# A transformer layer on one core: a fourth PSUM bank for the first group's experts, first loads on two queues, three items moved to the drain, and a new order of all items

## The reference

```python
x = x + attn(cond_moe(x))          # sparse experts, then banded linear attention, layer norm
x = x + ffn(cond2(x))              # 16-head attention with position bias and null key, then FFN

# cond_moe: 8 experts of 64 plus 2 shared, top 2 by routing
logits = (x @ wt.T + repeat(cond @ wg.T)) / 2 ; scores = softmax(logits)
y = sum_top2(w_e * ((leaky(x @ gate_e) * (x @ up_e)) @ down_e)) + shared(x)
# attn: qkv = y @ W + b ; out = (q k^T / scale * band) v ; layer norm
# cond2: xn = ln(x) * g ; q, k l2-normed ; softmax(8 q k^T + bias, causal, mask) v ; ln(out @ Wout)
# ffn: h = silu(z w1) * (z w2) ; h = gelu(h h1) ; h = gelu(h h2) ; h @ w3
```

## Time and profile before

| | |
|---|---|
| median of 3 runs | 853.04 us (852.45 to 853.72) |
| the profiled execution | 853.67 us, its span 851.9 us |
| PE busy | 800.9 us (94%), 5368 matmuls |
| PEld busy | 599.7 us (70%) |
| ACT busy | 603.0 us (71%) |
| DVE busy | 589.0 us (69%) |
| POOL busy | 447.4 us (53%) |
| DMA | 16.98 MB, mean 20 GB/s |
| mean granted clock | 0.992 |

### The profile page before, as it was taken

One profiled execution on the slowest core, in us unless ns is written; L12 is line 12 of the kernel. 1 busy time (PEld: TensorE's weight loads), 2 busy tenths in 40 slices (PEclk: granted clock), 3 DMA queues, 4 the chain that ended last, 5 costly groups with the idle time before them and its releaser, 6 DMA issues. The chain is left out here.

```text
span 851.9 us, 16700 instructions
## 1 busy us (share of the span) xinstructions
PE 800.9 (94%) x5368; PEld 599.7 (70%) x5368; DVE 589.0 (69%) x1581; ACT 603.0 (71%) x1649; POOL 447.4 (53%) x388
## 2 busy tenths in 40 slices
PE   5978879999999999999999999999999989999987
PEld 4756556678676777678676777778776766777777
DVE  5578878776767686776767586776767786664522
ACT  2314768588857888588866878588866978779944
POOL 3027874754558365754558364654558455944200
PEclk9989999999999999999999999999999999999999
DMA  7041100000010000100010000100010000000000
GB/s 245 1 156 35 63 14 4 2 2 2 1 41 2 1 2 2 42 1 2 2 42 1 2 1 2 41 1 1 1 42 1 2 1 2 13 2 1 13 7 7
DMA packets 15588, 16.98 MB, mean 20 GB/s; under 512 B 1408, under 2 KB 13072, under 8 KB 15120
## 3 DMA queue, kind: packets, MB, share of 16 engines
q1 hardware_dynamic: 15216, 15.27, 5.7%
q10 hardware_dynamic: 288, 0.66, 0.2%
HBM read 13.81 MB, written 2.11 MB: 19 GB/s over the span
## 5 line engine op out<-in xcount | busy, mean ns | idle before, releaser
L632 POOL TENSOR_TENSOR sb_sm<-sb_sm,sb_rden 128x512 f32<-128x512 f32 x128 | 135.9, 1068 | 209.0 <-DVE sb_rden L1097 209.0
L728 ACT ACTIVATE sb_sm<-sb_sm,sb_nmx 128x129 f32<-128x129 f32 x512 | 199.2, 393 | 26.7 <-DVE sb_nmx L1092 26.4
L1084 DVE SCALAR_TENSOR_TENSOR sb_sm<-ps_S,sb_rq,sb_biasm 128x129 f32<-128x129 f32 x512 | 140.9, 343 | 60.2 <-PE ps_S L1316 21.2
L625 POOL TENSOR_TENSOR sb_biasm<-sb_bias,sb_maskn 128x512 f32<-128x512 f32 x128 | 165.8, 1310 | 21.5 <-DVE sb_sm L1084 12.8
L615 POOL TENSOR_TENSOR sb_rq<-sb_qss,sb_mhalf 128x16 f32<-128x16 f32 x32 | 92.5, 2916 | 41.5 <-DVE sb_qss L1069 41.5
L728 ACT ACTIVATION_READ_ACCUMULATOR sb_sm<-sb_sm,sb_nmx 128x1 f32 x512 | 97.1, 190 | 0.0
L1316 PEld LDWEIGHTS ps_S<-sb_k,sb_qs 64*128 64x128 f32 x1024 | 64.8, 187 | 34.7 <-issue 32.9
L1316 PE MATMUL ps_S<-sb_k,sb_qs 64*128 64x129 f32 x1024 | 83.1, 291 | 6.5 <-DVE sb_sm L1084 6.5
L1092 DVE TENSOR_REDUCE sb_nmx<-sb_sm 128x4 f32<-128x516 f32 x128 | 85.8, 675 | 0.6
L735 ACT ACTIVATE sb_pT<-ps_T 128x512 f32<-128x512 f32 x128 | 75.0, 591 | 14.3 <-PE ps_T L1324 14.3
L1324 PE MATMUL ps_T<-sb_ident,sb_sm 128*128 128x128 f32 x512 | 76.8, 276 | 3.4 <-ACT sb_pT L735 2.4
(11 more groups left out here) (226 smaller groups left out, 1800.7 us busy)
## 6 DMA issues: line engine op xcount, KB each, us to landing
sb_xg<-in_xT SPq DMA_DIRECT2D x8, 256.0 KB, 4.2
sb_xs<-in_x SPq DMA_DIRECT2D x8, 256.0 KB, 3.8
sb_qs<-in_xT SPq DMA_DIRECT2D x1, 2048.0 KB, 10.8
sb_hA<-in_h SPq DMA_DIRECT2D x2, 1024.0 KB, 4.8
out_y<-sb_res SPq DMA_DIRECT2D x7, 256.0 KB, 2.6
sb_sm<-toeplitz SPq DMA_DIRECT2D x1, 1024.0 KB, 5.8
sb_rows<-in_rows SPq DMA_DIRECT2D x1, 648.0 KB, 6.8
sb_oT<-in_wq SPq DMA_DIRECT2D x1, 512.0 KB, 10.4
```

Source lines behind the costliest of these rows:

```text
L625: pool.tensor_tensor(biasm[:, heads, 1:NK], bias0[:, heads], maskn[:, j // 4].unsqueeze(1).broadcast_to([128, 4, S]), ALU.add)\
L632: pool.tensor_tensor(sm[:, heads, 1:NK], sm[:, heads, 1:NK], rden[:, heads].unsqueeze(2).broadcast_to([128, 4, S]), ALU.mult)\
L728: ins = act.activation(sm[:, h], sm[:, h], ACT.Exp, bias=nmx[:, h:h + 1], accum_out=den[:, h:h + 1])
L1084: ins = dve.scalar_tensor_tensor(sm[:, h], bank(g, "sim", n, odd)[:, m * NK:(m + 1) * NK], rq[:, k * HEADS + h:k * HEADS + h + 1], biasm[: ...
```

## The change

- PSUM: stage A of group 0 (it runs in the fill) takes its banks from a ring F, which is the ring M and the bank T1. `warm` uses T0.
- DMA: SP issues x's first group, then wg and wu, then cols and rows; condT, wgT and wt go to ScalarE's queue, where wg and wu were.
- GpSimd sets `eps` first and counts a semaphore of its own; ScalarE runs one copy of 128 x 1 on it, ahead of its wait for `cols`.
- `l3d.2`, `l3d.3` and `l4d.0` leave the last phase; `l3p.2`, `l3p.3` and `l4p.0` join the drain, on every engine that has a part in them.
- Every engine's list is in a new order in every phase. No other item is added or removed.

The diff, cut: of the 30 lists the ones below; the hunks behind them are whole.

```diff
@@ ORDER @@
     "pe fill": """
-        lg.0 warm.0-2 pb.0-1 warm.3-7 lg.1-2 rw.0 exp.0 lg.3-4 exp.1 lg.5 exp.2 lg.6-7 pb.2 warm.8 exp.3-4
-        warm.9 down.0 pb.3 warm.10-12 qkv.0 scores.0 warm.13 mix.0 warm.14 fl.0 warm.15 fl.1-2 warm.16 xnT.0
-        fl.3 q.0-2 warm.17 kv.0 q.3 qs.0-1 q.4-5 qs.2-3 q.6 qs.4 q.7 qs.5-7 warm.18 qst.0 warm.19-21 kT.0
+        lg.0 warm.0 pb.0 warm.1-5 pb.1 warm.6 lg.1-2 warm.7 rw.0 exp.0 lg.3-4 exp.1 lg.5 exp.2 lg.6 pb.2 lg.7
+        exp.3 warm.8 exp.4 down.0 warm.9 pb.3 warm.10 qkv.0 scores.0 mix.0 warm.11-13 fl.0-2 warm.14 fl.3 xnT.0
+        warm.15-16 q.0-2 kv.0 q.3 qs.0-2 q.4-7 qs.3-7 warm.17 qst.0 kT.0 warm.18-21
     """,
...
     "pe start": """
-        rw.0 sim.0 exp.0 sim.1 exp.1 sim.2 exp.2-3 PT.0 sim.3 PT.1 exp.4 PV.0 sim.4 PT.2 down.0 sim.5 PT.3 qkv.0
-        scores.0 PV.1 mix.0 PT.4 sim.6 PT.5-6 sim.7 PV.2 z.0-1 PT.7 sim.8 z.2 sim.9 PT.8-9 xnT.0 PV.3 PT.10
-        sim.10 q.0-1 sim.11 kv.0 q.2 PT.11 q.3 PT.12 PV.4 qs.0-2 q.4-5 z.3 q.6 qs.3 PT.13 z.4 qs.4-5 PV.5-6 q.7
-        PT.14 kT.0 PT.15 qs.6 z.5 qs.7 PV.7 qst.0 z.6-7
+        sim.0 rw.0 sim.1 exp.0-1 sim.2 exp.2 sim.3 exp.3 PT.0-1 exp.4 PV.0 sim.4 PT.2 down.0 PT.3 sim.5 PT.4
+        qkv.0 scores.0 PT.5 sim.6 PT.6 mix.0 PV.1 sim.7 z.0-1 PT.7 PV.2 sim.8 PV.3 z.2 PT.8 z.3 sim.9 PT.9 xnT.0
+        PV.4 PT.10 sim.10 q.0 kv.0 sim.11 PT.11 q.1-2 PT.12 q.3 PV.5 qs.0-2 z.4 q.4-5 PT.13 z.5 q.6-7 PT.14
+        qs.3-5 kT.0 PT.15 qs.6-7 PV.6-7 qst.0 z.6-7
     """,
...
     "pe steady": """
-        sim.0 rw.0 exp.0-1 sim.1 exp.2-3 sim.2 exp.4 down.0 PT.0 sim.3 zT.0 PT.1 qkv.0 l1.0 sim.4 l1.1 PT.2 l1.2
-        PT.3 PV.0-1 l1.3 sim.5 scores.0 z.0 l2.0-1 PT.4 sim.6 l2.2 PT.5-6 l2.3 mix.0 sim.7 l3.0-1 PT.7 l3.2
-        sim.8 PV.2-3 sim.9 z.1 PT.8 xnT.0 l3.3 PT.9 kv.0 q.0 PT.10 sim.10 q.1 z.2-3 q.2 PT.11 sim.11 PV.4-5
-        qs.0-1 q.3 PT.12 q.4 z.4 q.5 PT.13 l4.0 q.6 PV.6 PT.14 qs.2-4 q.7 kT.0 PT.15 z.5 qs.5-7 PV.7 qst.0 z.6-7
+        rw.0 sim.0 exp.0-1 sim.1 exp.2-3 sim.2 exp.4 down.0 PT.0 zT.0 sim.3 qkv.0 PT.1 l1.0-2 PT.2-3 l1.3 sim.4
+        PV.0-1 sim.5 scores.0 l2.0-2 sim.6 PT.4 mix.0 PT.5 l2.3 sim.7 z.0-1 PT.6 l3.0 PT.7 sim.8 PV.2-3 sim.9
+        z.2 PT.8 l3.1-2 xnT.0 PT.9 l3.3 PT.10-11 kv.0 q.0-2 sim.10 PV.4-5 sim.11 z.3 l4.0 q.3 PT.12 q.4 PT.13
+        z.4 q.5 PV.6 qs.0-3 PT.14 q.6-7 z.5 kT.0 PT.15 qs.4-7 PV.7 qst.0 z.6-7
     """,
...
     "pe last": """
-        sim.0 l3p.2 sim.1 l3p.3 sim.2 l4p.0 PT.0 zT.0 sim.3 PT.1 l1.0-1 sim.4 PT.2 l1.2-3 PV.0 sim.5 PT.3 l2.0-1
-        PT.4 l2.2 sim.6 PT.5 z.0 l2.3 sim.7 PV.1 PT.6 l3.0-1 PT.7 PV.2-3 z.1 sim.8 l3.2 z.2 sim.9 z.3 PT.8-9
-        l3.3 PT.10 sim.10 l4.0 PT.11 PV.4 sim.11 zTd.0 PV.5 z.4 l1d.0-1 PT.12 l1d.2-3 PT.13 z.5 l2d.0 PV.6 PT.14
-        l2d.1-3 z.6 l3d.0-1 PT.15 l3d.2-3 PV.7 l4d.0 z.7
+        sim.0 l3p.2 sim.1 l3p.3 sim.2 l4p.0 sim.3 PT.0 zT.0 PT.1-2 l1.0-2 PT.3 l1.3 sim.4 PV.0-1 sim.5 l2.0-2
+        z.0 PT.4 sim.6 PT.5 l2.3 PV.2 sim.7 PT.6 z.1 PT.7 z.2 sim.8 l3.0-1 PT.8 PV.3 sim.9 l3.2 PT.9 z.3 l3.3
+        PT.10 sim.10 PV.4 l4.0 PT.11-12 zTd.0 sim.11 PV.5 l1d.0 z.4 l1d.1 PT.13 l1d.2 PT.14 l1d.3 z.5 PV.6
+        l2d.0-2 PT.15 l2d.3 PV.7 z.6-7 l3d.0-1
     """,
...
     "pe drain": """
-        zT.0 l1.0-3 l2.0-3 l3.0-3 l4.0
+        l3p.2 zT.0 l3p.3 l1.0 l4p.0 l1.1-3 l2.0-3 l3.0-3 l4.0
     """,
...
     "act drain": """
-        zT.0 l1.0-1 h1.0 l1.2 h1.1-2 l1.3 h1.3 l2.0 h2.0 l2.1-2 h2.1-2 l2.3 h2.3 l3.0-3
+        l3p.2 zT.0 l3p.3 l1.0 h1.0 l1.1 h1.1 l1.2-3 h1.2-3 l2.0 h2.0 l2.1 h2.1 l2.2 h2.2 l2.3 h2.3 l3.0-3
     """,
...
     "dve fill": """
-        cg.0 rt.0 pb.0 wl.0 rt.1 pb.1 rt.2-4 pb.2 x0.0 rw.0 nk.0 pb.3 exp.0 nk.1 exp.1-2 rt.5 exp.3 pl.0 rt.6
-        exp.4 rt.7 down.0 rt.8 maskn.0 qkv.0 scores.0 xl.0 pl.1 mix.0 pl.2 ln1.0 rt.9 ln2.0 xnT.0 q.0-2 kv.0
-        q.3-4 kT.0 pl.3 ssq.0 q.5 ssc.0 q.6-7 vs.0
+        cg.0 rt.0 pb.0 nk.0 pb.1 wl.0 rt.1-4 pb.2 x0.0 rw.0 exp.0 pb.3 nk.1 exp.1 pl.0 exp.2 rt.5 exp.3 rt.6-7
+        exp.4 rt.8 down.0 rt.9 qkv.0 scores.0 mix.0 pl.1 ln1.0 pl.2 ln2.0 xnT.0 maskn.0 pl.3 q.0-2 kv.0 q.3-5
+        kT.0 ssq.0 ssc.0 q.6-7 xl.0 vs.0
     """,
...
     "dve steady": """
-        rw.0 xl.0 ln3.0 sim.0 exp.0-1 sim.1 exp.2 max.0 exp.3 inv.0 max.1-2 sim.2 exp.4 max.3 inv.1 zT.0 down.0
-        zl.0 sim.3 qkv.0 inv.2 l1.0 inv.3 l1.1 sim.4 h1.0 max.4 l1.2 h1.1 max.5 l1.3 scores.0 h1.2-3 inv.4 max.6
-        inv.5 sim.5 h2.0 inv.6 sim.6 h2.1 max.7 h2.2 mix.0 h2.3 sim.7 max.8 inv.7 max.9 ln1.0 inv.8 max.10 sim.8
-        inv.9 ln2.0 max.11 maskn.0 inv.10 xnT.0 sim.9 kv.0 max.12 inv.11 sim.10 max.13 sim.11 q.0 inv.12 q.1
-        inv.13 max.14 q.2-3 max.15 inv.14 q.4 kT.0 inv.15 q.5 l4.0 q.6 ssq.0 ssc.0 q.7 vs.0
+        rw.0 xl.0 ln3.0 sim.0 exp.0-1 sim.1 exp.2 max.0 exp.3 max.1 inv.0 sim.2 max.2 inv.1 max.3 exp.4 zT.0
+        inv.2 down.0 zl.0 inv.3 qkv.0 sim.3 l1.0-1 h1.0 max.4 h1.1 l1.2-3 sim.4 h1.2-3 max.5-6 sim.5 inv.4
+        scores.0 inv.5 max.7 h2.0 sim.6 h2.1 max.8 inv.6 h2.2-3 inv.7 sim.7 max.9 mix.0 max.10 sim.8 inv.8 ln1.0
+        max.11 ln2.0 inv.9-11 sim.9 xnT.0 max.12 kv.0 maskn.0 sim.10 q.0 inv.12 max.13 q.1 max.14 q.2 inv.13
+        sim.11 l4.0 max.15 inv.14 kT.0 q.3-5 inv.15 ssq.0 q.6 ssc.0 q.7 vs.0
     """,
...
     "dve last": """
-        sim.0 max.0 sim.1 ln3.0 max.1 inv.0 max.2 sim.2 inv.1 max.3 zT.0 l4p.0 zl.0 inv.2 sim.3 l1.0-1 h1.0
-        inv.3 sim.4 h1.1 l1.2-3 max.4 h1.2 max.5 h1.3 max.6 sim.5 inv.4-5 sim.6 h2.0-1 inv.6 max.7 h2.2-3 max.8
-        sim.7 max.9 inv.7 sim.8 max.10 inv.8-9 max.11 inv.10 ln3d.0 sim.9 max.12 inv.11 sim.10 max.13 inv.12
-        max.14 zTd.0 l4.0 zld.0 inv.13 sim.11 l1d.0-1 h1d.0 inv.14 h1d.1 l1d.2-3 max.15 h1d.2-3 h2d.0-3 inv.15
-        l4d.0
+        sim.0 max.0 ln3.0 sim.1 max.1 sim.2 inv.0 max.2-3 inv.1 zT.0 inv.2 l4p.0 zl.0 sim.3 l1.0 inv.3 l1.1
+        h1.0-1 max.4 l1.2 sim.4 l1.3 h1.2-3 max.5 sim.5 inv.4 max.6 inv.5-6 h2.0 max.7 h2.1-2 sim.6 inv.7 sim.7
+        max.8-9 h2.3 inv.8 max.10 sim.8 inv.9 max.11 sim.9 inv.10 max.12 inv.11 ln3d.0 sim.10 max.13 inv.12
+        max.14 inv.13 zTd.0 zld.0 l4.0 inv.14 sim.11 l1d.0-1 h1d.0-1 l1d.2-3 max.15 h1d.2-3 inv.15 h2d.0-3
     """,
...
     "pool start": """
-        pn.0 bias.4 pn.1 bias.5 pn.2-3 bias.6-7 xb.0 bias.8 pn.4 bias.9 pn.5 bias.10 pn.6 bias.11 ln1.0 bias.12
-        pn.7 bias.13-14 pn.8 ln2.0 pn.9 bias.15 pn.10-11 bias+.0 pn.12 bias+.1 pn.13 kv.0 pn.14-15 qn.0 bias+.2
-        qn.1-3 bias+.3
+        bias.4 pn.0-1 bias.5 pn.2 bias.6 pn.3 bias.7-9 pn.4-5 xb.0 pn.6 bias.10-12 ln1.0 pn.7 bias.13 pn.8
+        bias.14 ln2.0 pn.9-12 bias.15 pn.13 kv.0 pn.14 bias+.0 pn.15 bias+.1 qn.0-1 bias+.2 qn.2 bias+.3 qn.3
     """,
...
     "pool steady": """
-        zT.0 pn.0 xb.0 pn.1 bias.4-6 pn.2 bias.7-8 pn.3 bias.9 pn.4-6 bias.10 ln1.0 bias.11 pn.7 bias.12 ln2.0
-        bias.13 pn.8-9 bias.14-15 pn.10-11 bias+.0-1 pn.12-14 bias+.2-3 kv.0 pn.15 qn.0-3
+        zT.0 pn.0 bias.4-5 xb.0 pn.1 bias.6 pn.2 bias.7-8 pn.3 bias.9-11 pn.4-6 bias.12 pn.7 ln1.0 pn.8 ln2.0
+        pn.9 bias.13 pn.10 bias.14 pn.11 bias.15 bias+.0 kv.0 pn.12 bias+.1 pn.13 bias+.2 pn.14-15 qn.0-3
+        bias+.3
     """,
...
     "sp last": """
-        l4p.0 l4.0 l4d.0
+        l4p.0 l4.0
     """,
...
     "sp drain": """
-        l4.0
+        l4p.0 l4.0
     """,
...
@@ -220,13 +219,17 @@
         "kv": "M", "q": "M", "ssq": "", "kT": "M", "sim": "SS", "PT": "T", "PV": "T", "zT": "M",
         "l1": "MM", "l2": "M", "l3": "M", "l4": "M"}
 BANKS = {"M": 3, "S": 2, "T": 2}
-
-
-def uses(step, k):
+RINGS = {ring: [(ring, i) for i in range(n)] for ring, n in BANKS.items()}
+RINGS["F"] = RINGS["M"] + [("T", 1)]
+
+
+def uses(step, g, k):
+
     step = PART.get(step, step)
     if step == "qs":
         return "S" if k == 0 else ""
-    return "MM" if (step, k) == ("exp", NX - 1) else USES.get(step, "")
+    rings = "MM" if (step, k) == ("exp", NX - 1) else USES.get(step, "")
+    return rings.replace("M", "F") if g == 0 and STAGE[step] == "A" else rings
 
 
 PHASES = {-1: "fill", 0: "start", NG - 2: "seventh", NG - 1: "last", NG: "drain"}
@@ -247,10 +250,10 @@
 
 def bank_plan():
 
-    last, turn, plan = {}, {r: 0 for r in BANKS}, {}
+    last, turn, plan = {}, {r: 0 for r in RINGS}, {}
     for step, g, k in passes("pe"):
-        for n, ring in enumerate(uses(step, k)):
-            bank = (ring, turn[ring] % BANKS[ring])
+        for n, ring in enumerate(uses(step, g, k)):
+            bank = RINGS[ring][turn[ring] % len(RINGS[ring])]
             turn[ring] += 1
             plan[step, g, k, n] = bank, last.get(bank)
             last[bank] = step, g, k, n
@@ -333,7 +336,7 @@
         bs = sb("bs", [128, 3, GB, 6])
         mv = sb("mv", [128, 3, GB, 2])
         ve = sb("ve", [128, 3, GB])
-        idle = sb("idle", [128, 1])
+        idle, idle_act = sb("idle", [128, 1]), sb("idle_act", [128, 1])
         rstd = sb("rstd", [128, 3, GB])
 
         qs = sb("qs", [128, NP, GT])
@@ -387,7 +390,7 @@
```

(16 more changed lines are left out.)

80 lines of the change are left out of this document (40 added, 40 removed).

## The result

The new kernel takes 823.4 us, the median of 4 runs (822.76 to 824.58), against 853.09 before: a ratio of 0.9654, 95% interval 0.9637 to 0.967, or 29.7 us less. The forecast was 836.5 with a range of 827 to 847, so the direction was right and the size was not. The profiled execution took 822.76 us, its span 821.0.

What follows compares the result with a forecast made beforehand. TensorE's own 800.9 us of matmuls were taken as the bound, leaving 51 us idle and lower-clock stretches; -8.5 - 4.1 - 2.0 - 4.5 = -19.1, with +2.5 for new waits -16.6, gave 836.5 us, range 827 to 847.

Steps and rivals of the forecast that it cites:

- Steady stage and seventh, -8.5: Steady groups and seventh: waits before xnT, 1.57 us in five groups and 1.43 in the seventh, go, less a charge.
- 0.8 had been charged for all six: Steady groups and seventh: 0.8 us in all set against the gain for new lateness at qkv and down.
- Start stage, -4.1: Start stage: the 2.41 us wait before sim.5 and 1.7 us lost to the lower clock behind it both go.
- I take these as even: Start stage: four further waits, 5.8 us in all, priced at no gain, with VectorE nearly full there.
- Fill, -2.0: Fill: warm items -1.0 and -0.5, pl.3 and q.5 moved away -1.2, flips +0.7, loads and fourth bank 0.
- price of 0 for the loads: Fill: new queue order of first loads brings 0, bounds -3 to +0.5, as routing's end stays near 19.5.
- Last and drain, -4.5: Last stage and drain: three items moved into the drain gain 6.3 us, less 1.8 charged; bounds -7 to 0.
- the sum of 6.3: Drain: waits of 2.69 before zT, 1.08 before l1, 0.8 before the first silu, and 1.7 of lower clock go.
- the charge of 1.8: Drain: 1.8 us for l3p.3's gelu and the table load ahead of the first silu, and one more exp/gelu switch.
- if the softmax keeps up: Last stage: condition for z.7 coming 7.6 us of TensorE work earlier, with inv.15 now ahead of h2d.0-3.
- +2.5 for new waits: Whole kernel: 2.5 us added to the time for new waits among moved items that were not followed.
- Rival A: Whole kernel: everything lands, with the start's 5.8 us and the fill's bounds, no new waits: 827 us; chance 0.13.

Runs made afterwards that it cites:

- b_steady: Kernel before with only the new lists of the five steady groups and the seventh: 844.50 us (0.9903).
- b_bias6: Kernel before with GpSimd's bias.6 put ahead of pn.3 in the start list, nothing else: 849.13 us (0.9954).
- b_loads: Kernel before with only the new first loads and the early ScalarE copy, no fourth bank, all lists as before: 849.37 us (0.9959).
- a_loads_before: New kernel with the first loads as before and without the early ScalarE copy: 825.68 us (0.9675).
- b_loads_noearly: Kernel before with the new order of the first loads on two queues, without the early ScalarE copy: 851.15 us (0.9984).
- b_move_end: Kernel before with l3d.2-3 and l4d.0 moved into the new drain lists and the end of the last lists in the new order: 846.59 us (0.9926).
- four one-phase kernels: Kernel before with one phase from the new kernel each: fill 848.75, start 845.68, steady with seventh 844.50, last with drain 845.85 us.
- a_nobank: New kernel without the fourth bank for group 0's projections, lists and loads unchanged: 823.81 us (0.9655).
- a_pn15: New kernel with GpSimd's pn.15 put ahead of bias+.0 in the start list: 820.80 us (0.9621).
- b_fill: Kernel before with the new fill lists, first loads and fourth bank, later lists as before: 848.75 us (0.995).
- b_start: Kernel before with only the new start lists, on all five engines: 845.68 us (0.9927).
- b_tail: Kernel before with only the new last and drain lists, l3d.2-3 and l4d.0 done in the drain: 845.85 us (0.9918).
- b_port: Kernel before with three steady items moved: VectorE's inv.9 behind ln2.0, GpSimd's pn.8 ahead of ln2.0, pn.9 ahead of bias.13: 847.52 us (0.9931).
- a_port: New kernel with GpSimd's bias.13 put ahead of pn.9 in the steady lists: 824.55 us (0.9657).
- b_fill_lists: Kernel before with only the new fill lists, loads and banks as before: 851.34 us (0.9981).
- b_start_peact: Kernel before with the new start lists on TensorE and ScalarE alone: 871.46 us (1.0213).

## Why the prediction was right or wrong

**The step that failed for the whole** is the sentence that a new order "can win only from the 51 us of idle time and from stretches at the lower clock", with "TensorE's own 800.9 us of matmuls" as a floor. Of the 30.9 us, 16.9 were idle time and 4.8 the lower clock. The other 9.2 us were busy time of the same matmuls at a granted clock of 1.00, and the sum had no term for it: 2.7 in the fill (where 20 warm matmuls alone take between 3.50 and 4.47 us from trace to trace), 1.4 in the start stage, 2.8 in the five steady groups, 1.0 in the seventh and 1.4 in the last phase. With the 2.5 us of reserve it makes 11.7 of the 14.3 us between forecast and result.

**Steady stage and seventh, -8.5: the cause right, the sum partly by luck** (-8.3 by `b_steady`). The cause, the size of the stretch and the cover were each shown by an edit of their own. But a new wait of 0.60 us a group appeared at `PV`, where I had guessed `qkv` or `down`. That is 3.0 us in five groups, and 0.8 had been charged for all six. The matmuls' busy time, for which nothing was put, gave 2.8 us back. The seventh gave 2.8 instead of 1.3: besides its 1.43, waits of 0.42, 0.57 and 0.27 us ahead of `PT` and the score matmuls are gone, with one of 0.28 left in their place, and 0.9 is busy time.

**Start stage, -4.1: mis-sized.** `b_bias6` measured the step that I priced, 3.7 us. Two terms beside it failed. "I take these as even" stood for the four further waits, 5.8 us. In the new profile six waits (0.19, 0.39, 0.19, 1.16, 0.34 and 0.25) add up to 2.5 us and one of 2.00 ahead of `PT.15` is new, against 6.5 us before with the small ones counted: 2.0 less. And nothing was put for a wait of 1.60 us at 84.82, inside `exp.1`, which is gone; the foreseen one ahead of `sim.1` came in its place, with 1.40. The rest, 1.4 us, is busy time at a granted clock of 1.00. The reason given for "even", VectorE nearly full, was no reason. It has as much work in the stage as before (61.07 us against 61.99) and is fuller (88% against 80%), and the stage is 7.8 us shorter.

**Fill, -2.0: wrong in its parts.** The failed step is the price of 0 for the loads. I argued that the routing waits for `rows`, landing at 10.3 "with the same bytes ahead of it". VectorE waits for `rows` in none of the traces of before, `b_loads` and after. It landed at 8.1 to 10.3 in the thirteen traces with the old loads and at 8.9 to 9.7 in the seven with the new. The routing follows the product of condT and wgT, and in `b_loads` it was done 1.7 us earlier with no list changed; in the new kernel it ended at 18.6 and not near 19.5. Part of that is chance: with the loads as before the product started between 6.3 and 7.2 in thirteen traces (6.6 in the mean), with the new ones between 5.1 and 5.5 in seven (5.3). The profile of before was one of the late ones. The 1.3 us between the means, and the 1.3 us of `a_loads_before`, are close to the 1.5 us of saved issue time that the rule of the Trainium skill (DMA: Bandwidth & Descriptors, section Issuing engines are not separate DMA queues) came to, which I had set beside my 0; the traces agree with the rule rather than with me. The medians of `b_loads` and `b_loads_noearly` gave more (3.2 and 1.9); what the rest is stays open. The lists gave 1.2 where 2.0 was put, and the fourth bank next to the nothing that was put.

**Last and drain, -4.5: the sum of 6.3 was right, the charge of 1.8 was not.** `b_move_end` measured 6.4. By the trace the phase's 7.0 are 4.0 of waits, 1.6 of the clock and 1.4 of other busy time. The first silu of the drain had a wait of 0.27 us and not "up to 0.8", and has 0.30 now. So the later gelu and the table load ahead of it cost next to nothing, since TensorE works on `l4p.0` meanwhile. The condition that I named in passing ("if the softmax keeps up") is worth more (3.9) than the move itself (2.5).

**+2.5 for new waits: not borne out.** It was put on top of the charges inside the terms, so the same caution was counted twice.

**The clock.** Behind waits, the trace of before has three stretches at the lower clock; weighing every microsecond's busy time with what the clock column lacks to 1.00 gives 6.3 us lost before and 1.5 after. The forecast counted two of the three (1.7 each), so the clock is 1.4 us of what it missed. The four one-phase kernels still lost 4.0 to 8.9 us each in their profiles, `a_nobank`, `a_loads_before` and `a_pn15` none. That is a likely reason why the parts add up to 3.1 us less than the whole, and not shown: it rests on one trace of each kernel, and by the same weighing the clock alone would leave 8.6 us (the four lost 3.8 more than four times the kernel before, the new kernel 4.8 less). What takes the other part back stays open.

Rival A's 827 (all lands, 0.13) was nearer than the forecast, but its terms did not come true one by one: it had 9.3 for the steady stage and the seventh (8.3 measured by `b_steady`), 9.9 for the start (7.2), 5 for the fill (4.1) and 4.5 for the drain (7.0).

## What to carry to other kernels

Don't take TensorE's busy time as a floor when its list is reordered: sum idle and busy time between the same two items in both traces. Don't call waits "even" because an engine beside them is full, and do not add a reserve on top of charges already made. Where VectorE and GpSimd both work at length on SBUF, look for the pair that runs at the same time, and let the one that nobody waits for take the block: this was one swap of two items, for 3.7 us and again for 2.6. Lists of several engines are one schedule: half of a good one cost four to five times what `bias.6` alone gained.

## What the runs showed of the hardware

**The same matmuls take less time in another order.** With TensorE's old steady list a group of 637 matmuls is busy for 94.5 to 94.6 us in five traces (before, `b_fill`, `b_start`, `b_tail`, `b_port`), with the new list for 93.9 to 94.3 in three (after, `b_steady`, `a_port`), at a granted clock of 1.00 in all. Over the five groups the 40 matmuls `yTh,wq2h` of the queries fall from 19.3 to 17.7 us, the 160 on `hT,heads` from 7.6 to 6.4 and the 80 on `hAh,h1h` from 33.6 to 32.5; those of `z` and `PV` gain 1.1 each. The ends of matmuls are modelled in a profile, but the periods bear it out (94.7 against 95.3 in `b_port`, at no less idle time). Which neighbour costs what no run shows.

**The same waits cost differently in two traces.** `b_fill` has in its start stage the waits of the kernel before, 5.7 us earlier: 1.79, 1.81 and 0.83 us at 115.67, 119.84 and 122.89; in the kernel before they are 1.79, 1.81 and 1.07 at 121.38, 125.56 and 128.59. Two stretches of `b_fill` and of the kernel before, at the same work:

```profile
118.00:123.00 5.00, 2.37 (x22) 1.84 (x22) 4.96 (x18) 2.99 (x11) 3.46 (x4) 0.84 0.18 52
123.00:128.00 5.00, 5.00 (x22) 2.73 (x24) 2.71 (x9) 1.69 (x5) 1.04 (x1) 0.50 0.00 0
```

```profile
124.00:129.00 5.00, 2.38 (x24) 2.05 (x24) 5.00 (x16) 2.71 (x11) 3.45 (x4) 1.00 0.18 52
129.00:134.00 5.00, 4.53 (x31) 2.62 (x31) 4.37 (x17) 3.61 (x12) 1.19 (x2) 1.00 0.00 0
```

One falls to 1.2 GHz and the other stays at 2.4. That loses 3.0 us with its edges, more than the 2.2 us that `b_fill` gave back in its start stage. The start of the stage, 5.6 us earlier, is what differs by the edit; that it is the reason is not shown, with one trace of each. Over all kernels most such stretches cost about 1.6 or about 3 us. The ten runs of `b_fill_lists` fall into two groups, 849.4 to 850.4 and 852.3 to 853.2. The five faster ones have mean granted clocks of 0.992 to 0.996, the five slower ones 0.990 each, so a longer time at the lower clock is likely what parts them.

**The clock column does not show everything.** The 20 warm matmuls took 4.47 us in `b_loads_noearly` and 3.50 in `b_loads` at a granted clock of 1.00 in both columns, and moved `rw` by 1.4 us with all other engines in step. The Trainium skill, TensorE: Matmul & The Clock Gate, says that how much of a kernel's start is slow varies from run to run; the two traces agree. Its figure for the cost, under 1% of the span, is of the start alone; over a whole run here the stretches at the lower clock cost 6.3 us in the kernel before (0.7%) and up to 15.7 us (`b_start_peact`, 1.8%).
